# Swapping the row-group and slab axes of two masked operand tiles in a fused attention and expert block

## The chip, the cores and the metric

The kernel runs on one core of one Trainium2 chip. The metric is the device time of one execution in microseconds; of several executions the median counts. The core has TensorE (matmul), VectorE, ScalarE, GpSimd, and SyncE, whose queue issues all DMAs of this kernel.

## The reference

For 32 sequences of 128 tokens and width 128, the block computes a gated cross-attention and then a gated mixture of eight experts. Cut to what matters:

```
q = heads(layernorm(x) @ Wq.T + bq); k = heads(ctx @ Wk.T + bk); v = heads(ctx @ Wv.T + bv)   # 16 heads of 8
scores = einsum("bhqd,bhkd->bhqk", q, k) / sqrt(8);  scores = where(mask, min, scores)
x = x + tanh(g_xattn) * (softmax(scores) @ v merged over heads @ Wo.T + bo)
w = relu(softmax(n @ Wg + bg) - sigmoid(n @ Wt + bt) / 8), normalised      # n = layernorm(x)
x = x + tanh(g_ffn) * sum_e w_e * (gelu(n @ W1_e + b1_e) @ W2_e + b2_e)    # 8 experts, 512 hidden
```

## The kernel before

The program has two stages. The first (to about 290 us) does everything up to the gate; the second (290 us to the end) does the experts, with 512 tokens at a time as the moving operand, and the diff touches nothing in it.

The first stage is a software pipeline over 16 groups of two sequences (`GB = 2`, `GT = 256` tokens). `body(it)` on each engine handles several groups at different depths; `loop` runs some bodies unrolled, some in a hardware loop. The order of work on each engine is written out by hand, and semaphores are the only thing between engines.

Heads are only 8 wide, so four heads share one 128-row operand. The 16 heads are 4 slabs (`SLABS`, index s) of 4 row groups (`ROWS`, index r): head r of slab s lives in partitions 32r to 32r+31, which hold the high and low float parts of its 8 components in three copies, and some helper rows. The projections end in `k_stack` and `q_stack`, each [128 partitions, slab, 256 tokens] of 4 bytes, written by VectorE (L681). To get the scores of the four heads of a slab by one matmul, the operand is spread out with zeros: `k_masked` and `q_masked` hold, for each r, only partitions 32r to 32r+31 of the stack, the others stay zero. Both are [128, 4, 4, 256]: 16 KB in a partition.

The spreading is done by DMA from SBUF to SBUF, four DMAs per tile and group, one for each r: 32 partitions for `k_masked` (L380), 24 for `q_masked` (L395). Then one DMA copies `k_stack` to `k_cur` (L396). SyncE issues these in order: the `max_rows(1)` DMA of the current group (L359), the four `k_masked` copies of the next, the load of `ctx_sb` (L384), the four `q_masked` copies, `k_cur`, `max_rows(0)`, and the loads of the mask and of expert weights (L405, L408). The `k_masked` copies wait until VectorE has written `k_stack` and TensorE has read the former `k_masked`.

TensorE uses them in `natural` (L1002: `q_stack` of one slab as weights, `k_masked` as the moving operand with 4 blocks of 128 tokens; L1003 adds the mask) and `transposed` (L994: `k_cur` as weights, `q_masked` moving; L995 adds the mask). `natural` gives scores with the queries in partitions, only so that VectorE can take the negated maximum of each row (L654, into `neg_max`). `max_split` (L663, L665) cuts the 16 maxima into a high and a low part, TensorE transposes them, ScalarE copies them to `maxT`, and `max_rows` (L359) writes them as two rows of `q_masked`, so that `transposed` gives scores less the maximum, with keys in partitions, ready for the exponential (L546) and for `values` (L1013). For each group there are 8 `natural` and 8 `transposed` calls.

Of the kernel before, what the change touches and what calls it, by code (L numbers as in the profile page):

```python
# [25 lines left out]
F32 = mybir.dt.float32  # L26
F32R = mybir.dt.float32r
# [7 lines left out]
P = 128  # L35
B, S, D = 32, 128, 128
H, HD = 16, 8
E, FF = 8, 512
TOK = B * S
GB = 2  # L40
GT = GB * S
NG = B // GB
SLABS, ROWS = 4, 4
# [42 lines left out]
def group_at(it, ahead):  # L86

    if isinstance(it, int):
        g = it + ahead
        return g if 0 <= g < NG else None  # L90
    return it + ahead


def gated_block(nc, a):
# [3 lines left out]
    with ctx:  # L98
        def sb(name, shape, dt, stack=ctx):
            return stack.enter_context(nc.sbuf_tensor(name, shape, dt))  # L100

        def sem(name):
            return ctx.enter_context(nc.semaphore(name))
# [14 lines left out]

        def sa(name, shape, dt):
            return sb(name, shape, dt, phase_a)  # L120
        k_masked = sa("k_masked", [P, ROWS, SLABS, GT], F32R)
        q_masked = sa("q_masked", [P, ROWS, SLABS, GT], F32R)
        k_stack = sa("k_stack", [P, SLABS, GT], F32R)
        q_stack = sa("q_stack", [P, SLABS, GT], F32R)
        k_cur = sa("k_cur", [P, SLABS, GT], F32R)
# [28 lines left out]
        mean_var = sa("mean_var", [P, GB, 2], F32)  # L154
        rstd = sa("rstd", [P, GB], F32)
        power = sa("power", [P, B], F32)
        neg_max = sa("neg_max", [P, GB, ROWS, SLABS], F32)
        max_parts = sa("max_parts", [P, GB, 2 * H], F32R)
        maxT = sa("maxT", [2 * H, GT], F32R)
        headsT = sa("headsT", [P, GB, 2 * P], F32)  # L160
# [76 lines left out]
        km_in = sem("km_in")  # L237
        kcur_in = sem("kcur_in")
        qm_in = sem("qm_in")
        max_in = [sem("max0_in"), sem("max1_in")]  # L240
        maxhigh_done = [sem("max0_high_done"), sem("max1_high_done")]
# [41 lines left out]
        def settle(eng):  # L283

            eng.sem_inc(waited, 1)

        def misc_wait_full(eng, what, it):
            k = bank_of(what)
            eng.wait_ge(misc_full[k], fills(what, it))

        def misc_wait_read(eng, what, it):
            k = bank_of(what)
            eng.wait_ge(misc_read[k], fills(what, it))
# [8 lines left out]
        def wait_count(eng, s, n):  # L302
            if not (isinstance(n, int) and n <= 0):
                eng.wait_ge(s, n)

        def fill_of(group, b, s):

            return group * (GB * SLABS // 2) + (b * (SLABS // 2) + s // 2 + 1)
# [25 lines left out]
        def _(sp):  # L334
# [21 lines left out]
            sp.dma_start(x_all[:, 4 * GB:, :], a["x"][4 * GB * S:, :].rearrange("(b p) d -> p b d", p=P)).then_inc(x_rest_in, 16)  # L356

            def max_rows(b):
                sp.dma_start(q_masked[24:26, :, :, b * S:(b + 1) * S].rearrange("p r s q -> p (r s) q").bitcast(F32),  # L359
                             maxT[:, b * S:(b + 1) * S].bitcast(F32)).then_inc(max_in[b], 16)  # L360

            def body(it):
                if (g := group_at(it, 0)) is not None:
                    sp.wait_ge(maxT1_done, g + 1)
                    settle(sp)
                    max_rows(1)
                if (g := group_at(it, 1)) is not None:

                    misc_wait_read(sp, "p01", it - 1)
                    settle(sp)  # L370
                    misc_wait_read(sp, "p23", it - 1)
                    settle(sp)
                    if isinstance(g, int) and g == 0:
                        sp.wait_ge(pad_done, 2)
                    else:
                        sp.wait_ge(scoresN_full[1], fill_of(g - 1, GB - 1, SLABS - 1))
                        settle(sp)
                    for r in range(ROWS):
                        rows = slice(32 * r, 32 * r + 32)
                        sp.dma_start(k_masked[rows, r, :, :].bitcast(F32), k_stack[rows, :, :].bitcast(F32)).then_inc(km_in, 16)  # L380
                if (g := group_at(it, 3)) is not None and not (isinstance(g, int) and g == 0):
                    misc_wait_full(sp, "inputs", it)
                    settle(sp)
                    sp.dma_start(ctx_sb[:], ctx_v[g] if isinstance(g, int) else ctx_v[bass.ds(g, 1)]).then_inc(ctx_in, 16)  # L384
                if (g := group_at(it, 1)) is not None:
                    misc_wait_read(sp, "p45", it)
                    settle(sp)
                    misc_wait_read(sp, "p67", it)
                    settle(sp)
                    if not (isinstance(g, int) and g == 0):  # L390
                        sp.wait_ge(scoresT_full[1], fill_of(g - 1, GB - 1, SLABS - 1))
                        settle(sp)
                    for r in range(ROWS):
                        rows = slice(32 * r, 32 * r + 24)
                        sp.dma_start(q_masked[rows, r, :, :].bitcast(F32), q_stack[rows, :, :].bitcast(F32)).then_inc(qm_in, 16)  # L395
                    sp.dma_start(k_cur[:].bitcast(F32), k_stack[:].bitcast(F32)).then_inc(kcur_in, 16)  # L396
                    misc_wait_read(sp, "max0", it)
                    settle(sp)
                    max_rows(0)
                if (g := group_at(it, 2)) is not None and not (isinstance(g, int) and g == 0):  # L400
                    sp.wait_ge(masknxt_done, g)
                    settle(sp)
                    sp.wait_ge(maskcur_done, g)
                    settle(sp)
                    sp.dma_start(mask_words[:], mask_v[g] if isinstance(g, int) else mask_v[bass.ds(g, 1)]).then_inc(mask_in, 16)  # L405
                    sp.wait_ge(wsplit_done, g)
                    settle(sp)
                    sp.dma_start(w_raw[:], a["w_ffn"][g] if isinstance(g, int) else a["w_ffn"][bass.ds(g, 1)]).then_inc(w_in, 16)  # L408
            loop(sp, body)

            out_v = a["out"].rearrange("(g t p) d -> g p t d", p=P, t=TPB)
# [226 lines left out]
        def _(dve):  # L638
# [12 lines left out]

            def max_slab(group, b, s):
                dve.wait_ge(scoresN_full[s % 2], fill_of(group, b, s))
                nc.vector.tensor_reduce(neg_max[:, b, :, s],  # L654
                                        scores[:, 2 + s % 2, :].rearrange("p (r k) -> p r k", k=S),
                                        AX.X, ALU.max, negate=True).then_inc(scoresN_read[s % 2], 1)

            def max_split(group, b):

                for u in range(2):  # L660
                    dve.wait_ge(scoresN_read[u], fill_of(group, b, SLABS - 1))
                flat = neg_max[:, b, :, :].rearrange("p r s -> p (r s)")
                nc.vector.tensor_copy(max_parts[:, b, 0:H], flat).then_inc(maxhigh_done[b], 1)  # L663
                dve.wait_ge(maxhigh_done[b], group + 1)
                nc.vector.tensor_tensor(max_parts[:, b, H:2 * H], flat, max_parts[:, b, 0:H].bitcast(F32),  # L665
                                        ALU.subtract).then_inc(max_done[b], 1)

            def body(it):
# [90 lines left out]
                if (g := group_at(it, 1)) is not None:  # L759
                    max_slab(g, 1, 2)  # L760
                    max_slab(g, 1, 3)
                    max_split(g, 1)
# [96 lines left out]
        def _(pe):  # L859
            mm = nc.tensor.matmul  # L860

            def body(it):
# [26 lines left out]
                if (g := group_at(it, 0)) is not None:  # L889
                    transposed(g, 0, 2)  # L890
# [35 lines left out]
                if (g := group_at(it, 1)) is not None:  # L926
                    natural(g, 0, 2)
# [62 lines left out]
            def transposed(cur, b, s):  # L990

                wait_count(pe, scoresT_read[s % 2], fill_of(cur, b, s) - 1)
                dst = scores[:, s % 2, :].rearrange("p (r q) -> p r q", r=ROWS)
                mm(dst, k_cur[:, s, b * S:(b + 1) * S], q_masked[:, :, s, b * S:(b + 1) * S], start=True, stop=False)  # L994
                mm(dst, mask_cur[:, b, :], masked_ident[:].unsqueeze(1).to_broadcast([P, ROWS, P]),  # L995
                   start=False, stop=True).then_inc(scoresT_full[s % 2], 1)

            def natural(nxt, b, s):

                wait_count(pe, scoresN_read[s % 2], fill_of(nxt, b, s) - 1)  # L1000
                dst = scores[:, 2 + s % 2, :].rearrange("p (r k) -> p r k", r=ROWS)
                mm(dst, q_stack[:, s, b * S:(b + 1) * S], k_masked[:, :, s, b * S:(b + 1) * S], start=True, stop=False)  # L1002
                mm(dst, masked_ident[:], mask_nxt[:, b, :].unsqueeze(1).to_broadcast([P, ROWS, S]),  # L1003
                   start=False, stop=True).then_inc(scoresN_full[s % 2], 1)

# [129 lines left out]
```

## Time and profile before

| | us |
|---|---|
| median of 3 executions | 684.37 |
| lowest, highest | 682.66, 685.3 |
| the profiled execution, its own time | 685.3 |
| its span in the trace | 683.5 |
| TensorE busy in the span | 633.4 (93%) |
| VectorE busy | 532.4 (78%) |
| ScalarE busy | 432.8 (63%) |

The profile gives for each engine the busy time and, for each instruction, start, duration and what released it. Two cautions: a matmul's start is a record but its end is modelled, and neighbouring matmuls overlap, so that the rate of TensorE is read from the distance of starts a whole pattern apart, not from a mean duration. And a DMA row of SyncE's queue is the issuing only; the transfer lands later, and the views give that time apart.

### The profile page before, as it was taken

What the parts mean: (1) busy time and instruction counts of PE and PEld (TensorE: products, weight loads), DVE (VectorE), ACT (ScalarE), POOL (GpSimd) and SP (SyncE); (2) the same over time, 40 slices, a digit from 0 to 9 for tenths busy, and PEclk for the clock granted to TensorE, in tenths of its full rate; (3) what the DMA queues carried; (4) which work ended last, traced back from release to release, by engine and by line L of the source; (5) the groups of instructions that cost most, each with busy time, mean ns of one, the idle gap of its engine ahead of it and who ended that gap; (6) DMA issues with size and microseconds to landing.
All of it is one profiled execution on the core that took longest, in us unless ns stands there. A gap on an engine that the chain in (4) does not pass through costs nothing.

```text
span 683.5 us, 14449 instructions
## 1 busy us (share of the span) xinstructions
PE 633.4 (93%) x3944; PEld 478.2 (70%) x3944; DVE 532.4 (78%) x1083; ACT 432.8 (63%) x764; POOL 188.4 (28%) x242
## 2 busy tenths in 40 slices
PE   2899999999999999739999999999999999999996
PEld 2566666666666766427878878778788788787784
DVE  5778888899988888346877877868778778788686
ACT  3456666666666666418767757667576677675773
POOL 6224444444444443100230221212302202213022
PEclk9999999999999999959999999999999999999999
DMA  6544444444444444103121111111211211111110
GB/s 190 140 110 121 109 120 119 114 114 116 111 111 111 114 110 114 40 0 85 47 62 43 51 47 56 51 34 64 70 35 46 61 46 46 46 61 53 54 46 15
DMA packets 37386, 52.74 MB, mean 77 GB/s; under 512 B 9328, under 2 KB 20464, under 8 KB 37360
## 3 DMA queue, kind: packets, MB, share of 16 engines
q1 hardware_dynamic: 37360, 52.42, 27.8%
q8 instruction: 13, 0.21, 0.1%
q14 instruction: 13, 0.11, 0.1%
HBM read 26.58 MB, written 2.23 MB: 42 GB/s over the span
## 4 chain that ended last, share of the span: by engine, by line
PE 79%; DVE 8%; POOL 3%; DMA 3%; issue 2%; SPq 2%; ACT 2%; DVEq 0%; POOLq 0%; ACTq 0%
PE ps_y L1041 8%; PE ps_y L1043 8%; PE ps_y L1042 8%; PE ps_h L1061 8%; PE ps_h L1063 8%; PE ps_h L1062 8%; PE scores L994 5%; PE scores L995 4%; PE scores L1002 3%; PE scores L1003 3%; POOL yT L527 3%; DVE neg_max L654 3%; PE heads L1013 3%; PE misc L882 2%; PE misc L883 2%
## 5 line engine op out<-in xcount | busy, mean ns | idle before, releaser
L627 ACT ACTIVATE h_sb<-ps_h,b_sb 128x512 f32<-128x512 f32 x256 | 175.4, 689 | 116.2 <-PE ps_h L1063 103.6
L841 DVE TENSOR_TENSOR h_low<-h_sb,h_high 128x512 fp32r<-128x512 f32 x256 | 164.4, 682 | 0.0
L527 POOL TENSOR_TENSOR yT<-yT,weighted 128x512 f32<-128x512 f32 x56 | 72.3, 1292 | 309.2 <-DVE weighted L829 308.4
L837 DVE CAST h_high<-h_sb 128x512 fp32r<-128x512 f32 x128 | 86.8, 678 | 81.8 <-ACT h_sb L627 81.8
L1041 PE MATMUL ps_y<-h_high,w_high 128*128 128x512 f32 x256 | 102.2, 399 | 5.0 <-DVE h_low L841 5.0
L1061 PE MATMUL ps_h<-x_high,w_high 128*128 (+1 forms) x256 | 101.9, 398 | 0.1
L1043 PE MATMUL ps_y<-h_high,w_low 128*128 128x512 f32 x256 | 101.3, 396 | 0.0
L1042 PE MATMUL ps_y<-h_low,w_high 128*128 128x512 f32 x256 | 100.9, 394 | 0.0
L1063 PE MATMUL ps_h<-x_high,w_low 128*128 (+1 forms) x256 | 100.8, 394 | 0.0
L1062 PE MATMUL ps_h<-x_low,w_high 128*128 (+1 forms) x256 | 100.0, 391 | 0.0
L654 DVE TENSOR_REDUCE neg_max<-scores 128x4 f32<-128x512 f32 x128 | 83.6, 685 | 12.5 <-PE scores L1003 11.7
L632 ACT ACTIVATE h_high<-ps_h,b_sb 128x512 fp32r<-128x512 f32 x128 | 87.5, 684 | 0.0
L546 ACT ACTIVATE probs<-scores 128x512 f32<-128x512 f32 x128 | 72.9, 596 | 22.9 <-PE scores L995 20.6
L560 ACT ACTIVATE part<-misc,bqk_low,low_rows_sb 128x256 fp32r<-128x256 f32 x128 | 65.5, 565 | 34.5 <-PE misc L884 34.5
L1002 PE MATMUL scores<-k_masked,q_stack 128*128 128x512 f32 x128 | 63.6, 526 | 2.3 <-DMA k_masked<-k_stack 2.3
L994 PE MATMUL scores<-q_masked,k_cur 128*128 128x512 f32 x128 | 60.8, 503 | 4.4 <-DMA k_cur<-k_stack 1.9
L1041 PEld LDWEIGHTS ps_y<-h_high,w_high 128*128 128x128 f32 x256 | 48.0, 188 | 20.0 <-DVE h_low L841 5.6
L1061 PEld LDWEIGHTS ps_h<-x_high,w_high 128*128 128x128 f32 x256 | 48.5, 189 | 11.6 <-issue 0.5
L1062 PEld LDWEIGHTS ps_h<-x_low,w_high 128*128 128x128 f32 x256 | 48.5, 190 | 11.3
L1063 PEld LDWEIGHTS ps_h<-x_high,w_low 128*128 128x128 f32 x256 | 48.3, 188 | 11.1
L1043 PEld LDWEIGHTS ps_y<-h_high,w_low 128*128 128x128 f32 x256 | 48.1, 188 | 11.2
L1042 PEld LDWEIGHTS ps_y<-h_low,w_high 128*128 128x128 f32 x256 | 48.1, 188 | 9.8
(122 smaller groups left out, 990.7 us busy)
## 6 DMA issues: line engine op xcount, KB each, us to landing
w_row<-w_scratch SPq DMA_DIRECT2D x64, 256.0 KB, 3.2
k_masked<-k_stack SPq DMA_DIRECT2D x64, 128.0 KB, 2.4
k_cur<-k_stack SPq DMA_DIRECT2D x16, 512.0 KB, 3.0
q_masked<-q_stack SPq DMA_DIRECT2D x64, 96.0 KB
w_raw<-in_w_ffn SPq DMA_DIRECT2D x16, 256.0 KB, 2.7
ctx_sb<-in_ctx SPq DMA_DIRECT2D x16, 128.0 KB, 2.1
out_y<-y_out SPq DMA_DIRECT2D x8, 256.0 KB, 3.6
probs<-in_wqk SPq DMA_DIRECT2D x2, 256.0 KB, 3.1
```

What stands on the lines that cost most here:

```text
L527: nc.gpsimd.tensor_tensor(yT[:], yT[:], weighted[:, e % 2, :], ALU.add).then_inc(added, 1)
L627: nc.scalar.activation(h_sb[:, j % HBUF, :], ps_h[:, j % 4, :], ACT.Gelu_apprx_tanh, bias=b1_sb[:, j:j + 1]).then_inc(h_done, 1)
L632: nc.scalar.activation(h_high[:, j % HBUF, :], ps_h[:, j % 4, :], ACT.Gelu_apprx_tanh, bias=b1_sb[:, j:j + 1]).then_inc(high_even, 1)
L654: nc.vector.tensor_reduce(neg_max[:, b, :, s], scores[:, 2 + s % 2, :].rearrange("p (r k) -> p r k", k=S), AX.X, ALU.max, negate=True).the ...
L841: V.tensor_tensor(h_low[:, j % HBUF, :], h_sb[:, j % HBUF, :], h_high[:, j % HBUF, :].bitcast(F32), ALU.subtract).then_inc(low2_done, 1)
L994: mm(dst, k_cur[:, s, b * S:(b + 1) * S], q_masked[:, :, s, b * S:(b + 1) * S], start=True, stop=False)
L1041: mm(dst, w_high[:, E + e, cols], h_high[:, j % HBUF, :], start=(f == 0), stop=False)
L1042: mm(dst, w_high[:, E + e, cols], h_low[:, j % HBUF, :], start=False, stop=False)
L1043: mm(dst, w_low[:, E + e, cols], h_high[:, j % HBUF, :], start=False, stop=(f == FC - 1)).then_inc(w2_done, 1)
L1061: mm(dst, w_high[:, e, cols], xh, start=True, stop=False)
L1062: mm(dst, w_high[:, e, cols], xl, start=False, stop=False)
L1063: mm(dst, w_low[:, e, cols], xh, start=False, stop=True).then_inc(h_full, 1)
```

## The change

The two axes r and s of `k_masked` and `q_masked` change places: from [partition, r, s, token] to [partition, s, r, token]. Everything that indexes them follows: the spreading DMAs, the two matmuls, and `max_rows`. `neg_max` and so the order of the 16 maxima changes from (r, s) to (s, r), so that VectorE writes the four maxima of a slab side by side, and `max_rows` still writes 16 rows in the order of the tile. The alias `flat` in `max_split` goes, since `neg_max` is now flat.

For a matmul of slab s the four blocks of 128 tokens (512 bytes each) lay 4096 bytes apart and now lie 1024 bytes apart. For a spreading DMA the destination of one partition was one run of 4096 bytes and is now four runs of 1024 bytes, 4096 bytes apart; the source stays one run of 4096 bytes. No instruction is added, taken away or moved.

```diff
-        k_masked = sa("k_masked", [P, ROWS, SLABS, GT], F32R)
-        q_masked = sa("q_masked", [P, ROWS, SLABS, GT], F32R)
+        k_masked = sa("k_masked", [P, SLABS, ROWS, GT], F32R)
+        q_masked = sa("q_masked", [P, SLABS, ROWS, GT], F32R)
...
-        neg_max = sa("neg_max", [P, GB, ROWS, SLABS], F32)
+        neg_max = sa("neg_max", [P, GB, H], F32)
...
-                sp.dma_start(q_masked[24:26, :, :, b * S:(b + 1) * S].rearrange("p r s q -> p (r s) q").bitcast(F32),
+                sp.dma_start(q_masked[24:26, :, :, b * S:(b + 1) * S].rearrange("p s r q -> p (s r) q").bitcast(F32),
...
-                        sp.dma_start(k_masked[rows, r, :, :].bitcast(F32), k_stack[rows, :, :].bitcast(F32)).then_inc(km_in, 16)
+                        sp.dma_start(k_masked[rows, :, r, :].bitcast(F32), k_stack[rows, :, :].bitcast(F32)).then_inc(km_in, 16)
...
-                        sp.dma_start(q_masked[rows, r, :, :].bitcast(F32), q_stack[rows, :, :].bitcast(F32)).then_inc(qm_in, 16)
+                        sp.dma_start(q_masked[rows, :, r, :].bitcast(F32), q_stack[rows, :, :].bitcast(F32)).then_inc(qm_in, 16)
...
-                nc.vector.tensor_reduce(neg_max[:, b, :, s],
+                nc.vector.tensor_reduce(neg_max[:, b, ROWS * s:ROWS * s + ROWS],
...
-                flat = neg_max[:, b, :, :].rearrange("p r s -> p (r s)")
-                nc.vector.tensor_copy(max_parts[:, b, 0:H], flat).then_inc(maxhigh_done[b], 1)
+                nc.vector.tensor_copy(max_parts[:, b, 0:H], neg_max[:, b, :]).then_inc(maxhigh_done[b], 1)
...
-                mm(dst, k_cur[:, s, b * S:(b + 1) * S], q_masked[:, :, s, b * S:(b + 1) * S], start=True, stop=False)
+                mm(dst, k_cur[:, s, b * S:(b + 1) * S], q_masked[:, s, :, b * S:(b + 1) * S], start=True, stop=False)
...
-                mm(dst, q_stack[:, s, b * S:(b + 1) * S], k_masked[:, :, s, b * S:(b + 1) * S], start=True, stop=False)
+                mm(dst, q_stack[:, s, b * S:(b + 1) * S], k_masked[:, s, :, b * S:(b + 1) * S], start=True, stop=False)
```

On SyncE's queue, at the start of the second group's work, this is all that differs. The name before the arrow is what is written, the figures are partitions by the runs' dimensions, in elements of 4 bytes:

```order
-L380 DMA k_masked<-k_stack 32x1024 x4
+L380 DMA k_masked<-k_stack 32x4x256 x4
 L384 DMA ctx_sb<-in_ctx 128x2x128
-L395 DMA q_masked<-q_stack 24x1024 x4
+L395 DMA q_masked<-q_stack 24x4x256 x4
 L396 DMA k_cur<-k_stack 128x1024
 L359 DMA q_masked<-maxT 2x16x128
```

The order is the same; the spreading DMAs have become patterns of three dimensions, and the `max_rows` DMA has kept its form.

## Rows read from the trace of the kernel before

**Rows 1.** Page, part 1: busy time, share of the span, instructions of each engine.

```profile
PE 633.4 (93%) x3944; PEld 478.2 (70%) x3944; DVE 532.4 (78%) x1083; ACT 432.8 (63%) x764; POOL 188.4 (28%) x242
```

**Rows 2.** Busy time by stretches: projection-and-attention stage, expert stage; columns in the first line.

```profile
core 0: us, PE busy (x) PEld busy (x) DVE busy (x) ACT busy (x) POOL busy (x), PEclk, DMA share, GB/s
100.00:140.00 40.00, 39.40 (x365) 27.52 (x363) 35.43 (x94) 27.97 (x57) 16.19 (x25) 1.00 0.43 112
290.00:683.00 393.00, 368.90 (x1588) 294.09 (x1588) 295.66 (x481) 252.33 (x391) 73.77 (x58) 0.97 0.16 49
```

**Rows 3.** Page, part 5: groups of instructions; last numbers are busy us, mean ns.

```profile
L841 DVE TENSOR_TENSOR h_low<-h_sb,h_high 128x512 fp32r<-128x512 f32 x256 | 164.4, 682 | 0.0
...
L1061 PE MATMUL ps_h<-x_high,w_high 128*128 (+1 forms) x256 | 101.9, 398 | 0.1
...
L654 DVE TENSOR_REDUCE neg_max<-scores 128x4 f32<-128x512 f32 x128 | 83.6, 685 | 12.5 <-PE scores L1003 11.7
...
L1002 PE MATMUL scores<-k_masked,q_stack 128*128 128x512 f32 x128 | 63.6, 526 | 2.3 <-DMA k_masked<-k_stack 2.3
L994 PE MATMUL scores<-q_masked,k_cur 128*128 128x512 f32 x128 | 60.8, 503 | 4.4 <-DMA k_cur<-k_stack 1.9
```

**Rows 4.** TensorE in order of time, attention: start us, duration us, engine, line.

```profile
120.35 0.50 PE L994 MATMUL scores<-q_masked,k_cur 128*128 128x512 f32 x1
120.69 0.39 PE L995 MATMUL scores<-masked_ident,mask_cur 128*128 128x512 bf16 x1
120.73 0.58 PE L1002 MATMUL scores<-k_masked,q_stack 128*128 128x512 f32 x1
121.16 0.39 PE L1003 MATMUL scores<-mask_nxt,masked_ident 128*128 128x512 bf16 x1
121.20 0.58 PE L1002 MATMUL scores<-k_masked,q_stack 128*128 128x512 f32 x1
...
122.58 0.58 PE L1002 MATMUL scores<-k_masked,q_stack 128*128 128x512 f32 x1
```

**Rows 5.** TensorE in order of time, expert stage, same columns.

```profile
499.98 0.39 PE L1061 MATMUL ps_h<-x_high,w_high 128*128 x1
500.21 0.39 PE L1062 MATMUL ps_h<-x_low,w_high 128*128 x1
...
505.50 0.39 PE L1061 MATMUL ps_h<-x_high,w_high 128*128 x1
```

**Rows 6.** Time line of the same iteration, the rows of SyncE's DMA queue.

```profile
116.16 2.48 SPq L380 DMA_DIRECT2D k_masked<-k_stack  x4
...
126.93 0.69 SPq L359 DMA_DIRECT2D q_masked<-maxT  x1
```

**Rows 7.** Line 380, k_masked copies: issue ns min/median/max, and below landings.

```profile
L380 SPq DMA_DIRECT2D k_masked<-k_stack x64: 562/582/649, 17.1 to 265.1; - x64
...
DMA to landing us min/median/max: 2.3/2.4/3.7
```

**Rows 8.** Time line of a later iteration: SyncE's copies and the matmul that needs them.

```profile
263.20 2.46 SPq L380 DMA_DIRECT2D k_masked<-k_stack  x4
...
267.61 0.58 PE L1002 MATMUL scores<-k_masked,q_stack 128*128 128x512 f32 x1
```

**Rows 9.** Waits, 20 to 280 us: waiter <- awaited: us total, times, longest.

```profile
PE scores L1002 <- DMA k_masked<-k_stack: 2.3, 2, 1.7
...
PE scores L994 <- DMA k_cur<-k_stack: 1.9, 2, 1.1
```

**Rows 10.** Chain that ended last, first 60 us: start us, us, what.

```profile
17.06 0.65 SPq L380
...
19.02 2.44 DMA k_masked<-k_stack
...
34.01 3.73 DMA k_masked<-k_stack
...
39.99 0.81 SPq L395
...
43.16 3.52 DMA k_cur<-k_stack
...
47.07 0.47 PE scores L994
```

**Rows 11.** Issues of lines 395, 396, 408, 427: ns min/median/max, first and last start.

```profile
L395 SPq DMA_DIRECT2D q_masked<-q_stack x64: 713/725/1722, 20.5 to 272.3; - x64
...
L396 SPq DMA_DIRECT2D k_cur<-k_stack x16: 532/535/552, 23.7 to 273.0; - x16
...
L408 SPq DMA_DIRECT2D w_raw<-in_w_ffn x15: 345/346/532, 28.8 to 259.1; - x15
...
L427 SPq DMA_DIRECT2D out_y<-y_out x7: 406/407/431, 368.6 to 646.1; - x7
```

**Rows 12.** DMA view of 117.0 to 119.0 us: only k_masked copies under way.

```profile
DMA packets 120, 0.36 MB, mean 180 GB/s; under 512 B 32, under 2 KB 32, under 8 KB 120
...
q1 hardware_dynamic: 120, 0.36, 80.0%
```

**Rows 13.** DMA view of 127.0 to 128.1 us: mostly the k_cur copy.

```profile
DMA packets 89, 0.32 MB, mean 287 GB/s; under 512 B 12, under 2 KB 12, under 8 KB 89
...
q1 hardware_dynamic: 89, 0.32, 82.9%
```

**Rows 14.** DMA view of 119.8 to 122.5 us: the ctx_sb load, 512-byte rows.

```profile
DMA packets 289, 0.14 MB, mean 50 GB/s; under 512 B 32, under 2 KB 288, under 8 KB 289
...
q1 hardware_dynamic: 289, 0.14, 17.6%
```

**Rows 15.** Page, part 6: DMA issues: count, KB each, median us to landing.

```profile
k_cur<-k_stack SPq DMA_DIRECT2D x16, 512.0 KB, 3.0
```

**Rows 16.** Time line at a k_cur copy and its first matmul.

```profile
126.21 0.54 SPq L396 DMA_DIRECT2D k_cur<-k_stack  x1
...
130.20 0.47 PE L994 MATMUL scores<-q_masked,k_cur 128*128 128x512 f32 x1 [0.17 <-issue]
```

More of the change, by code:

```diff
@@ L661, in max_split @@
                     dve.wait_ge(scoresN_read[u], fill_of(group, b, SLABS - 1))
-                flat = neg_max[:, b, :, :].rearrange("p r s -> p (r s)")
-                nc.vector.tensor_copy(max_parts[:, b, 0:H], flat).then_inc(maxhigh_done[b], 1)
+                nc.vector.tensor_copy(max_parts[:, b, 0:H], neg_max[:, b, :]).then_inc(maxhigh_done[b], 1)
                 dve.wait_ge(maxhigh_done[b], group + 1)
-                nc.vector.tensor_tensor(max_parts[:, b, H:2 * H], flat, max_parts[:, b, 0:H].bitcast(F32),
+                nc.vector.tensor_tensor(max_parts[:, b, H:2 * H], neg_max[:, b, :], max_parts[:, b, 0:H].bitcast(F32),
                                         ALU.subtract).then_inc(max_done[b], 1)
```

## The prediction

> **What bounds the kernel now.** Part 1 of the page gives TensorE 93% of the span, VectorE 78% [rows 1]. The busy time by stretches then splits this: in the first stage TensorE shows 39.40 of 40 us busy at the full granted clock (1.00), in the expert stage 368.90 of 393, and no line of the expert stage is touched [rows 2]. So whatever the change does is done before 290 us, and there it counts if it alters how fast TensorE streams, or makes it wait.
>
> The costliest groups hold a lure. The matmul that reads `k_masked` is given with a mean of 526 ns and the one that reads `q_masked` with 503, while a matmul of the same 512 columns in the expert stage, whose moving operand is one plain run, has 398 [rows 3]. Both slow ones are just those whose operand the change packs closer. But ends are modelled, so the rate has to be read from starts. In the attention stage a pair (masked operand, then mask) starts at 120.73, 121.20, ... 122.58: four pairs in 1.85 us, 0.462 us a pair [rows 4]. In the expert stage 24 matmuls start from 499.98 to 505.50: 0.230 us each, 0.460 for two [rows 5]. The blocks 4096 bytes apart therefore stream as fast as a plain run; the 526 ns is a start that is logged early, 0.04 us behind the mask matmul, and waits in the pipe.
>
> The third view is SyncE's queue beside TensorE. Four `k_masked` copies are issued from 116.16 on for 2.48 us, so the last starts near 118.04 [rows 6]; landing takes 2.4 us in the median [rows 7], hence 120.44. The first matmul that needs them starts at 120.73 [rows 4]: a slack of 0.29 us. From first issue to that matmul it is 4.57 us here; over the 14 groups behind the start-up it is about that in twelve, and 4.41 in the two tightest, of which one is shown, 263.20 to 267.61 [rows 8]: a slack of 0.13. The views of waits say the same from the other side: only 2 waits on these copies, 2.3 us in all, and 2 on `k_cur` [rows 9]. Those lie in the start-up, where the chain that ended last goes through the copies three times: 17.06 to 21.46, 32.15 to 37.74, and 39.99 to 46.68 with `k_cur` behind the `q_masked` copies [rows 10].
>
> **The change part by part.** *The matmuls* (128 of each kind): at most they could gain the 0.0025 us by which a pair is slower than two plain ones, x256 = 0.6 us, less than what two decimals can carry; a loss has no reason, since a plain run (block distance 512 bytes) and a distance of 4096 stream alike and 1024 lies between. I take 0.
>
> *VectorE's reduction*: it wrote 4 maxima 16 bytes apart and now side by side. It takes 685 ns; a subtraction that writes 512 elements in a run takes 682 [rows 3]. What the scatter costs is 3 ns, x128 = 0.4 us at most, and only a part of it is waited for. `max_split` reads and writes 16 values in a run before and after, and the `max_rows` DMA keeps its form. I take 0 for these.
>
> *The spreading DMAs* (64 + 64) are what really changes: a partition's 4096 bytes go in four runs of 1024. Two terms, the issue and the transfer.
>
> Issue: 0.582 us for a `k_masked` copy [rows 7]. The nearest rows on runs: a load with one run of 2 KB in each of 128 partitions takes 346 ns to issue, the store of four runs of 512 bytes each 406 [rows 11]: 384 more runs for 0.06 us. Upward the slowest form of this kernel is the 24-partition copy with 725 ns [rows 11], whose length I can't lay to runs. `max_rows` was issued in 0.69 [rows 6] with 32 runs of 512 bytes, 0.11 above. Downward, the 128-partition copy with 4 KB runs takes 535 and the one with 2 KB runs 346, so that shorter runs might save 0.19. I take +0.06, nearest in what differs; the ends are -0.19 and +0.11. Three issues lie ahead of the last: +0.18 us.
>
> Transfer: over 117.0 to 119.0 us the 16 engines are 80.0% busy and move 120 packets, 32 of them the small ones under 512 bytes: 0.80 x 16 x 2.0 us / 88 = 0.29 us for 4 KB [rows 12]. With `k_cur`, over all 128 partitions, it is 0.829 x 16 x 1.1 / 77 = 0.19 us [rows 13]. A copy within 32 partitions is thus held by something other than the engine itself. Pieces of 512 bytes take 0.176 x 16 x 2.7 / 257 = 0.030 us [rows 14], so 4 KB in eight such pieces 0.24, and in four of 1 KB at most that. Against 0.19 this is up to +0.05 for each row of 4 KB; an engine has two rows (32 partitions over 16 engines), +0.10 a copy, and if two engines that wait for each other both pay it, +0.19. If the pieces fit under the 0.29 that a row takes anyway, it is 0. I take +0.05, the middle of 0 and the plain +0.10. It doesn't add up over the four copies while issuing (0.64) is slower than moving (0.58 + 0.05). By the same row a faster issue would bring little: with 0.39 the engines, at 0.58 a copy, become the limit, so the batch ends 3 x 0.04 = 0.12 us earlier at the most.
>
> What the Trainium skill makes of these terms stands by itself. [...] The rule that speaks against the change is in the Trainium skill's "Perfetto Trace Analysis", section "Optimizing DMA Performance": large descriptors are what matters where DMA binds. [...] "SBUF — State Buffer" of the Trainium skill, section "Door 1: The DMA port swizzle", gives 32 partitions only 8 of 16 ports; the trace agrees (0.29 us for 4 KB against 0.19).
>
> **The sum.** The last copy lands x = 0.18 + 0.05 = 0.23 us later. In 12 steady groups that is under the slack of 0.29: 0. In two it exceeds 0.13 by 0.10: +0.2. In the start-up the chain runs through three batches: 3 x 0.23 = +0.7. `k_cur` in steady state: it lands 3.0 us after its issue [rows 15], so that the one of 126.21 is there at 129.2, and its matmul starts at 130.20 [rows 16]; four slower issues ahead (0.24) stay hidden. VectorE's writing of the next stacks comes far behind. Total +0.9 us on the profiled execution's 685.3, that is 686.2; the median of the runs stands 0.9 below that execution, so the forecast for the median is **685.3 us**. Bounds: x = -0.12 gives -0.4 (684.0); x = 0.33 + 0.19 = 0.52 gives 12 x 0.23 + 2 x 0.39 + 3 x 0.52 = +5.1 (689.5).
>
> **The rivals.** (1) *Late copies slow every iteration*: the mechanism just priced, past its threshold. Cost is 17x - 3.7 for x above 0.29, so it passes 0.5% (3.4 us) at x = 0.42, and with x = 0.52 the time is **689.5**. For it: a steady slack of only 0.29, engines 80% busy in the batch, and no steady wait that would absorb a delay of TensorE. Against: both terms must stand near their upper ends. Should issuing go to 725 ns, x is 0.43 + 0.10, much the same time. (2) *The masked matmuls really are slowed by the distance of their blocks*, and fall to 398 ns: 128 x 128 ns + 128 x 105 ns = 29.8 us, **654.6**. For it only the means; against it the starts, which leave nothing to gain. (3) *The DMAs get cheaper*, because long runs were what made issuing slow (535 against 346 ns): the transfers then bind, -0.4 us, **684.0**, which can't be told from no change. That the change doesn't do what it says is excluded, as SyncE's order shows the new forms.
>
> **How the numbers follow.** About 0.5% (3.4 us) is what a measurement of this kernel can tell from no change. The forecast (x between 0 and 0.42, 684.4 to 687.8) has 0.67, the cheaper DMAs 0.14, late copies 0.13, faster matmuls 0.04, and 0.02 for something unseen, split evenly. So faster 0.05, same 0.81, slower 0.14. The range runs from 682.5, the cheaper DMAs less the 1.7 us by which the lowest run stands under the median, to 689.0, most of the late-copies case; the matmul case is left out.
>
> **What would show it.** Starts of pairs 0.46 us apart as before, with the means of L1002 and L994 about where they are; packets of 1 KB in place of 4 KB, some 10,700 more in all; L380's issue near 0.64 us and landings at 2.4 to 2.5; iterations of 16.34 us as before (the nine from 116.16 to 263.20, [rows 6, 8]). New steady waits of L1002 on the `k_masked` copies would show rival 1; a pair under 0.45 us, rival 2; issuing under 0.5 us, rival 3. The forecast is wrong if the distance of blocks acts on something that starts of matmuls don't show, or if a copy of four runs is issued in another way than the rows compared here.

## The result and the profile after

The changed kernel is slower: a median of 689.77 us against 683.51, a ratio of 1.0091 with a 95% interval of 1.0068 to 1.0113. That is +6.3 us where +0.9 was forecast, and beyond the upper end of the range, 689.0.

Page of the changed kernel, part 5 (groups, mean ns after the busy time) and part 6 (DMA issues, last number the median landing). They answer to [rows 3, 15]:

```profile
L1060 PE MATMUL ps_h<-x_high,w_high 128*128 (+1 forms) x256 | 101.7, 397 | 0.0
...
L654 DVE TENSOR_REDUCE neg_max<-scores 128x4 f32<-128x512 f32 x128 | 83.7, 685 | 14.2 <-PE scores L1002 13.1
...
L993 PE MATMUL scores<-q_masked,k_cur 128*128 128x512 f32 x128 | 60.7, 503 | 8.4 <-issue 4.7
L1001 PE MATMUL scores<-k_masked,q_stack 128*128 128x512 f32 x128 | 62.9, 521 | 3.6 <-DMA k_masked<-k_stack 3.6
...
k_masked<-k_stack SPq DMA_DIRECT2D x64, 128.0 KB, 2.5
k_cur<-k_stack SPq DMA_DIRECT2D x16, 512.0 KB, 3.1
```

The line numbers of this file are one lower behind line 662, so that L1001 and L1002 are `natural`, L993 and L994 `transposed`. The matmuls take what they took (521 and 503 ns against 526 and 503), the reduction too (685). What has grown most is the idle time of TensorE before L993: 8.4 us where it was 4.4. Its largest part, 4.7 us, carries the name "issue", that is, no releaser that the trace could name. In the kernel before, that part was 0.5 us, as the view of the attention lines has it:

```profile
L994 PE MATMUL scores<-q_masked,k_cur 128*128 128x512 f32 x128 | 60.8, 503 | 4.4 <-DMA k_cur<-k_stack 1.9 <-DMA q_masked<-maxT 0.9 <-issue 0.5
```

The issue times of the copies, from the views of lines 380, 395 and 396 of the changed kernel (ns min/median/max), answer to [rows 7, 11]:

```profile
L380 SPq DMA_DIRECT2D k_masked<-k_stack x64: 587/612/757, 17.2 to 269.8; - x64
```

```profile
L395 SPq DMA_DIRECT2D q_masked<-q_stack x64: 778/788/1800, 20.7 to 278.9; - x64
...
L396 SPq DMA_DIRECT2D k_cur<-k_stack x16: 554/558/567, 24.1 to 279.7; - x16
```

The time line of one steady iteration of the changed kernel (start us, duration us; SPq is SyncE's DMA queue, PEld TensorE's weight load, which starts with its matmul or just ahead of it), to be laid beside [rows 4, 6, 16]:

```profile
116.98 2.61 SPq L380 DMA_DIRECT2D k_masked<-k_stack  x4
...
121.77 0.19 PEld L1001 LDWEIGHTS scores<-k_masked,q_stack 128*128 128x128 f32 x1 [0.18 <-issue]
...
123.99 3.39 SPq L395 DMA_DIRECT2D q_masked<-q_stack  x4
...
127.43 0.56 SPq L396 DMA_DIRECT2D k_cur<-k_stack  x1
...
128.18 0.68 SPq L359 DMA_DIRECT2D q_masked<-maxT  x1
...
131.36 0.19 PEld L993 LDWEIGHTS scores<-q_masked,k_cur 128*128 128x128 f32 x1 [0.46 <-issue]
...
132.60 0.67 SPq L359 DMA_DIRECT2D q_masked<-maxT  x1
...
133.78 0.66 SPq L380 DMA_DIRECT2D k_masked<-k_stack  x1
```

The same iteration of the kernel before, weight loads and issues that the rows ahead don't show:

```profile
120.70 0.19 PEld L1002 LDWEIGHTS scores<-k_masked,q_stack 128*128 128x128 f32 x1
...
123.03 3.14 SPq L395 DMA_DIRECT2D q_masked<-q_stack  x4
...
130.17 0.19 PEld L994 LDWEIGHTS scores<-q_masked,k_cur 128*128 128x128 f32 x1 [0.23 <-issue]
...
131.40 0.67 SPq L359 DMA_DIRECT2D q_masked<-maxT  x1
...
132.59 0.57 SPq L380 DMA_DIRECT2D k_masked<-k_stack  x1
```

Cut at five of these events, an iteration reads as follows (us, each stretch the difference of two starts):

| stretch | before | after |
|---|---|---|
| first `k_masked` issue to its first matmul's weight load | 4.54 | 4.79 |
| to the first `q_masked` issue | 2.33 | 2.22 |
| to the `max_rows(0)` issue | 3.90 | 4.19 |
| to the first `q_masked` matmul's weight load | 3.24 | 3.18 |
| to the next `k_masked` issue | 2.42 | 2.42 |
| iteration | 16.43 | 16.80 |

The events follow one another in a ring: the first `q_masked` matmul is followed by the issue of `max_rows(1)` after 1.23 us (1.24 in the changed kernel), and that by the next `k_masked` batch after 1.19 (1.18). Two stretches grew, +0.25 at the `k_masked` batch, of which 0.11 is given back in the next stretch, and +0.29 in the `q_masked` batch; the others differ by 0.06 at most. Over nine iterations the mean went from 16.37 us (`k_masked` issues from 83.36 to 230.67) to 16.81 (83.39 to 234.64), 0.44 us more each.

Laid over the whole profile, the account is this. Up to the third `k_masked` batch (49.63 us before, 49.03 after) the changed kernel was 0.6 us ahead; over the 13 iterations from there to the last batch (263.20 and 267.82) it lost 5.2 us; behind that batch it lost another 1.7, and this makes the 6.3 us between the spans. So the steady loss is most of it, 0.40 us an iteration with the last ones. The first and the last part hold one late landing each, of which more below.

### The profile page after: what moved, and what is told of

Its sections match the earlier page's. It is cut to its first block, busy times and chain, and to the rows that moved or that the text cites. A ratio compares the mean times of both kernels' runs of the same rounds, so it can differ in the third digit from the quotient of the medians.

```text
span 689.8 us, 14449 instructions
## 1 busy us (share of the span) xinstructions
PE 635.0 (92%) x3944; PEld 479.0 (69%) x3944; DVE 534.3 (77%) x1083; ACT 432.7 (63%) x764; POOL 188.1 (27%) x242
## 3 DMA queue, kind: packets, MB, share of 16 engines
HBM read 26.58 MB, written 2.23 MB: 42 GB/s over the span
## 4 chain that ended last, share of the span: by engine, by line
PE 79%; DVE 8%; issue 3%; POOL 3%; DMA 3%; SPq 2%; ACT 2%; DVEq 0%; POOLq 0%; ACTq 0%
PE ps_y L1040 8%; PE ps_y L1042 8%; PE ps_y L1041 8%; PE ps_h L1062 8%; PE ps_h L1060 8%; PE ps_h L1061 8%; PE scores L993 5%; PE scores L994 4%; PE scores L1001 4%; PE scores L1002 3%; POOL yT L527 3%; DVE neg_max L654 3%; PE heads L1012 3%; PE misc L881 2%; PE misc L882 2%
## 5 line engine op out<-in xcount | busy, mean ns | idle before, releaser
L993 PE MATMUL scores<-q_masked,k_cur 128*128 128x512 f32 x128 | 60.7, 503 | 8.4 <-issue 4.7
L1001 PE MATMUL scores<-k_masked,q_stack 128*128 128x512 f32 x128 | 62.9, 521 | 3.6 <-DMA k_masked<-k_stack 3.6
```

The costliest lines, as they stand in the source:

```text
L993: mm(dst, k_cur[:, s, b * S:(b + 1) * S], q_masked[:, s, :, b * S:(b + 1) * S], start=True, stop=False)
L1001: mm(dst, q_stack[:, s, b * S:(b + 1) * S], k_masked[:, s, :, b * S:(b + 1) * S], start=True, stop=False)
```

## The experiments

All kernels below were timed in five rounds beside the kernel before, whose median was 682.78 us beside e1 to e4, 683.12 beside e5 to e8 and 683.55 beside e9 and e10; differences and ratios are to these. The theories at the start: both batches arrive late and each costs something (theory T), or one of them alone (rivals K and Q), or the matmuls stream slower (rival M). A mean iteration is again that of nine in the steady loop.

**One operand at a time.** e1 gives the new order to `k_masked` only (the index of its matmul, left out here, follows):

```diff
-        k_masked = sa("k_masked", [P, ROWS, SLABS, GT], F32R)
+        k_masked = sa("k_masked", [P, SLABS, ROWS, GT], F32R)
...
-                        sp.dma_start(k_masked[rows, r, :, :].bitcast(F32), k_stack[rows, :, :].bitcast(F32)).then_inc(km_in, 16)
+                        sp.dma_start(k_masked[rows, :, r, :].bitcast(F32), k_stack[rows, :, :].bitcast(F32)).then_inc(km_in, 16)
```

> The kernel before, with the new axis order for k_masked alone. Theory T (both batches of copies come late: the k_masked batch lands beyond its slack by some 0.2 us an iteration, and the max_rows(0) DMA, queued behind the slower q_masked batch, by another 0.2): about half of the 6.3 us, 686 to 687.5. Rival Q (the delay comes from the q_masked batch alone, since the 0.29 us of slack before the k_masked matmul still covers it): no change in the steady iterations, 683.5 to 684.5. Rival K (the k_masked batch alone): 689 to 690. Rival M (the matmuls stream slower at 1024 bytes distance, not the DMAs): half of it, and pairs of matmuls more than 0.46 us apart.

Measured: 686.08 us, ratio 1.0045 (1.0028 to 1.0062). e2 is the complement:

> The changed kernel with k_masked put back to the old axis order: only q_masked (and the order of the maxima) is new. Theory T: the other half, 686 to 687.5, with the idle time before the first q_masked matmul of a group near 0.4 us where it was 0.17. Rival Q: all of it, 689 to 690. Rival K: 683.5 to 684.5. If both batches simply queue behind one another and either alone is absorbed, e1 and e2 together fall short of 6.3 us.

Measured: 688.96 us, ratio 1.0087 (1.0071 to 1.0103). Neither is nothing, so both theories of one batch alone fall; but e2 is above what theory T gave it. The `q_masked` batch by itself costs nearly as much as both together in time, and the two don't add up (+3.3 and +6.2 us against +6.3). The time line of an iteration of e2:

```profile
151.32 2.47 SPq L380 DMA_DIRECT2D k_masked<-k_stack  x4
...
155.88 0.19 PEld L1001 LDWEIGHTS scores<-k_masked,q_stack 128*128 128x128 f32 x1
...
158.20 3.44 SPq L395 DMA_DIRECT2D q_masked<-q_stack  x4
...
162.42 0.67 SPq L359 DMA_DIRECT2D q_masked<-maxT  x1
...
165.58 0.19 PEld L993 LDWEIGHTS scores<-q_masked,k_cur 128*128 128x128 f32 x1 [0.49 <-issue]
```

The first stretch is that of the kernel before (4.56), the `q_masked` batch has all the growth (158.20 to 162.42, 4.22 for 3.90), and the matmul follows `max_rows(0)` after 3.16 us, as in the changed kernel. In e1 it is the other way round: 4.85 in the first stretch, 3.94 in the third. Mean iterations: 16.58 (e1), 16.70 (e2), 16.81 (both), that is +0.21 and +0.33 against +0.44. Here too the parts come to more than the whole, by 0.10 us; why is open.

**A plain run for the moving operand, shorter runs for the DMA.** e3 is the changed kernel with the following edit; the spreading DMA, left out here, follows it with eight runs of 512 bytes in a partition:

```diff
-        k_masked = sa("k_masked", [P, SLABS, ROWS, GT], F32R)
+        k_masked = sa("k_masked", [P, SLABS, GB, ROWS, S], F32R)
...
-                mm(dst, q_stack[:, s, b * S:(b + 1) * S], k_masked[:, s, :, b * S:(b + 1) * S], start=True, stop=False)
+                mm(dst, q_stack[:, s, b * S:(b + 1) * S], k_masked[:, s, b, :, :], start=True, stop=False)
```

> The changed kernel with k_masked laid out as slab, sequence, row group, token: the moving operand of a k_masked matmul is one plain run of 512 elements, and a partition's row is copied in eight runs of 512 bytes. If pieces cost time (theory T), the k_masked batch issues and lands still later by about as much as from one run to four, 0.1 to 0.4 us an iteration: 691 to 695. If the distance of blocks in the moving operand costs anything, the pairs of L1001 and L1002 get closer than 0.46 us and the time falls to under 689. If neither, 689.8.

Measured: 696.01 us, ratio 1.0187 (1.0163 to 1.0212), a little above the expected 691 to 695. TensorE's time line of e3 has, where the operand is one run of 512 elements:

```profile
126.03 0.58 PE L1001 MATMUL scores<-k_masked,q_stack 128*128 128x512 f32 x1
...
127.42 0.58 PE L1001 MATMUL scores<-k_masked,q_stack 128*128 128x512 f32 x1
```

Three pairs in 1.39 us, 0.463 a pair: the same as with blocks 4096 bytes apart (0.462), and as in the changed kernel, where they are 1024 apart and three pairs take 1.38 us:

```profile
122.16 0.58 PE L1001 MATMUL scores<-k_masked,q_stack 128*128 128x512 f32 x1
...
123.54 0.58 PE L1001 MATMUL scores<-k_masked,q_stack 128*128 128x512 f32 x1
```

With that the rival of matmuls slowed by the distance is out. The landings of line 380 in e3, after 2.4/2.5/4.3 in the changed kernel and [rows 7] before:

```profile
DMA to landing us min/median/max: 2.5/2.8/4.4
```

Issuing hardly grew from four runs to eight (median 612 to 619 ns), landing did by 0.3 us, and the first stretch went to between 5.10 and 5.19. The mean iteration is 17.16. So shorter runs make the transfer's end later as well; at four runs it was 0.1.

**Taking the queue in front of max_rows(0) away.** e4 (changed kernel) and e5 (kernel before) have the one edit

```diff
+                    sp.dma_start(k_cur[:].bitcast(F32), k_stack[:].bitcast(F32)).then_inc(kcur_in, 16)
                     for r in range(ROWS):
                         rows = slice(32 * r, 32 * r + 24)
...
-                    sp.dma_start(k_cur[:].bitcast(F32), k_stack[:].bitcast(F32)).then_inc(kcur_in, 16)
```

> The changed kernel with the k_cur copy issued ahead of the four q_masked copies, so that the max_rows(0) DMA is no longer queued behind its 512 KB. Theory T: max_rows(0) and the last q_masked copy land earlier, the idle time before the first q_masked matmul goes, and the share of the q batch (about 3 us) comes back: 685.5 to 687.5. Rival K: nothing changes, 689.8. If k_cur's 512 KB only push the q_masked copies back by as much, nothing changes either, but then the idle time stays.

Measured: 682.85 us, ratio to the kernel before 0.9996 (0.9982 to 1.0011): more than expected, the whole loss is gone. The mean iteration is 16.39.

> The kernel before with k_cur issued ahead of the q_masked copies. If the first q_masked matmul of a group was waiting for max_rows(0) already in the kernel before (3.1 to 3.2 us from that issue to the matmul in every kernel that shows an idle time there), the wait shrinks a little and the time falls by what it was late, 0 to 0.2 us an iteration: 680.5 to 683. If there was a slack there, nothing changes: 683.

Measured: 680.32 us, ratio 0.9951 (0.9932 to 0.9970), by a hair below the range that a late gate was given. The kernel before was thus itself held up at this wait. e5's time line:

```profile
120.69 0.51 SPq L393 DMA_DIRECT2D k_cur<-k_stack  x1
121.25 3.15 SPq L396 DMA_DIRECT2D q_masked<-q_stack  x4
...
124.58 0.68 SPq L359 DMA_DIRECT2D q_masked<-maxT  x1
...
127.50 0.19 PEld L994 LDWEIGHTS scores<-q_masked,k_cur 128*128 128x128 f32 x1
```

From the `max_rows(0)` issue to the weight load it is now 2.92 us, and 2.64 in e4, with no idle time ahead; in the steady iterations of every kernel that has idle time there it is 3.1 to 3.3. The time from issue to readiness is thus 3.1 to 3.3 us behind `k_cur`'s 512 KB, and at most 2.64 without them. In the last group of the kernel before `max_rows(1)` goes out with no large copy ahead of it, and there the trace does name it as what the matmul waits for; the chain that ended last gives its landing:

```profile
278.14 2.26 DMA q_masked<-maxT
```

The views don't give this landing for `max_rows(0)` in the steady loop, nor those of the `q_masked` copies. That the wait is for `max_rows(0)` and not for the last of these copies is argued: in e5 the copies go out later behind the first `k_masked` matmul than in the kernel before (2.87 us against 2.33), `max_rows(0)` at the same distance (6.20 against 6.23), and the `q_masked` matmul comes 0.35 us earlier. In either case it is the 512 KB of `k_cur` that hold the matmul up. The iteration of e5 is 16.18 us.

**Delaying without touching a layout.** e6 and e7 are the kernel before with four increments of a semaphore that nobody waits for, ahead of one batch:

```diff
+                    for _ in range(4):
+                        settle(sp)
                     for r in range(ROWS):
```

> The kernel before with SyncE held up by four semaphore increments (an estimated 0.2 to 0.28 us, from the 0.05 to 0.07 us between such rows) ahead of each k_masked batch; layouts and transfers as before. The slack of 0.29 us that the prediction read: no steady change, 683 to 684. Slack of 0.05 or less, because the waits and register work that follow the wait for the copies in the loop take the rest: 0.15 to 0.25 us an iteration, 685.5 to 687, and from the batch's first issue to the matmul about 4.56 us as before, with the whole iteration longer.

Measured: 686.47 us, ratio 1.0047 (1.0032 to 1.0062).

> The same four increments ahead of each q_masked batch. Zero slack at max_rows(0): 0.2 to 0.28 us in each of 15 iterations, 686 to 688, with the idle time before the first q_masked matmul near 0.45 us. A slack of a microsecond, as the prediction had it from k_cur's landing: 683.

Measured: 688.20 us, ratio 1.0069 (1.0047 to 1.0091), 0.2 above the range. The time line of e6, ahead of and behind a `k_masked` batch:

```profile
150.49 2.46 SPq L382 DMA_DIRECT2D k_masked<-k_stack  x4
...
155.02 0.19 PEld L1004 LDWEIGHTS scores<-k_masked,q_stack 128*128 128x128 f32 x1 [0.15 <-issue]
...
157.24 3.13 SPq L397 DMA_DIRECT2D q_masked<-q_stack  x4
```

The batch now follows the first `q_masked` matmul of the group before after 2.67 us where it was 2.42, a delay of 0.25; the `k_masked` matmul still comes 4.53 us behind the batch, so it moved by the full 0.25: no slack at this gate. The following stretch gave 0.11 back (2.22 for 2.33), just as in the changed kernel, and the mean iteration is 16.51, +0.14.

The 0.11 us are a slack one step further on. In all nine iterations of the kernel before, the `q_masked` batch goes out 6.87 to 6.89 us behind the `k_masked` batch, whether the matmul between them came after 4.54 us or after 4.67: something other than this matmul released it. In the changed kernel and in e6 it goes out 2.21 to 2.23 us behind the matmul each time, which has become the later of the two. What the other one is, no run here shows.

e7 in the same way:

```profile
149.34 2.48 SPq L380 DMA_DIRECT2D k_masked<-k_stack  x4
...
156.44 3.13 SPq L397 DMA_DIRECT2D q_masked<-q_stack  x4
...
160.33 0.69 SPq L359 DMA_DIRECT2D q_masked<-maxT  x1
...
163.47 0.19 PEld L996 LDWEIGHTS scores<-q_masked,k_cur 128*128 128x128 f32 x1 [0.37 <-issue]
```

The `q_masked` batch goes out 7.10 us behind the `k_masked` batch, 0.22 later than before, and this comes through whole: the mean iteration is 16.59, +0.22, with 3.14 us from `max_rows(0)` to the matmul and 0.37 us idle ahead of it. Both matmuls stood without slack in the kernel before. This is shown without a layout, a run length or a matmul being different.

**What lies between landing and matmul.** e8 is the changed kernel with

```diff
-                    pe.wait_ge(km_in, g * (ROWS * 16) + ROWS * 16)
                     misc_wait_read(pe, "p45", it)
                     misc_wait_read(pe, "p67", it)
                     pe.wait_ge(masknxt_done, g + 1)
+                    pe.wait_ge(km_in, g * (ROWS * 16) + ROWS * 16)
...
-                    pe.wait_ge(max_in[0], g * 16 + 16)
                     pe.wait_ge(maskcur_done, g + 1)
+                    pe.wait_ge(max_in[0], g * 16 + 16)
```

> The changed kernel with two waits of TensorE moved, each behind the other waits of its group: the one for the k_masked copies to just ahead of their first matmul, and the one for max_rows(0) behind that for the mask. If the register work of the waits behind them is what lies between landing and matmul (about 0.28 us at k_masked), some 0.1 to 0.25 us an iteration come back: 686 to 688.5. If the time after landing is the DMA's own (the semaphore's travel), nothing changes: 689.8.

Measured: 690.38 us, ratio 1.0105 (1.0083 to 1.0128): no gain, a miss. One iteration of e8:

```profile
134.14 2.62 SPq L380 DMA_DIRECT2D k_masked<-k_stack  x4
...
138.77 0.19 PEld L1001 LDWEIGHTS scores<-k_masked,q_stack 128*128 128x128 f32 x1
...
141.03 3.39 SPq L395 DMA_DIRECT2D q_masked<-q_stack  x4
...
145.21 0.68 SPq L359 DMA_DIRECT2D q_masked<-maxT  x1
...
148.47 0.19 PEld L993 LDWEIGHTS scores<-q_masked,k_cur 128*128 128x128 f32 x1 [0.55 <-issue]
```

The first stretch fell from 4.79 to 4.63, so the three waits that followed, with their register work, were worth 0.16 us between landing and matmul. But the second took 0.04 of it back (2.26 for 2.22): the `q_masked` batch is again 6.89 us behind the `k_masked` batch, where the other release holds it. And the fourth grew by 0.08 (3.26 for 3.18), for a reason that no run shows. The mean iteration is 16.72 where it was 16.81, a gain that the timing doesn't resolve.

e9 and e10 put only the wait for the `k_masked` copies last, and issue `k_cur` first, on either layout:

> The kernel before with k_cur issued ahead of the q_masked copies (as in e5) and TensorE's wait for the k_masked copies put behind the three other waits of its place. e8 shortened the stretch from the first k_masked issue to its matmul from 4.80 to 4.63 us, but lost it again at max_rows(0). With the max_rows(0) wait out of the way, a gate at k_masked that still binds would let 0.1 to 0.15 us an iteration through: 678 to 679.5. If TensorE's own work is what fills the iteration of 16.19 us in e5, nothing changes: 680.3.

Measured: 679.57 us, ratio 0.9949 (0.9935 to 0.9963). That lies between the two cases of the expectation, but the interval is that of e5 and the iteration is 16.19 us for 16.18: nothing beyond e5 is shown.

> The changed kernel with both edits. e4 stands at 682.85 with 4.85 us from issue to matmul. If k_masked's gate binds there, the moved wait gives back about 0.17 us an iteration: 680 to 681. If both layouts then run alike (within 0.5% of the kernel with the same edits and the old layout), the whole cost of the new layout was in the two gates and none in the matmuls.

Measured: 681.47 us, ratio 0.9958 (0.9938 to 0.9977), 0.5 us above the range, and below e4, whose interval (0.9982 to 1.0011) this one doesn't reach. So with the first `q_masked` matmul relieved, the `k_masked` gate of the new layout still cost something in e4 (its matmul idles 0.20 to 0.28 us each time, and the iteration is 16.39), and the moved wait took it off. The `k_masked` batches follow each other in e9 and e10 like this:

```profile
112.26 2.46 SPq L380 DMA_DIRECT2D k_masked<-k_stack  x4
...
128.45 2.47 SPq L380 DMA_DIRECT2D k_masked<-k_stack  x4
```

```profile
112.82 2.61 SPq L380 DMA_DIRECT2D k_masked<-k_stack  x4
...
129.01 2.62 SPq L380 DMA_DIRECT2D k_masked<-k_stack  x4
```

16.19 us an iteration in both, with batches that take 2.46 and 2.61 us to issue. Once neither gate is late, the two layouts have the same iteration, and their times can't be told apart (0.9949 and 0.9958, the intervals overlap). Over such an iteration TensorE is busy 16.05 of 16.19 us in e9 and 16.04 in e10, and no view names a wait of it; that its own chain is what is left fits this, but no run tries it. The lowest times of the study are those of e5 and e9, on the old layout, 0.5% below the kernel before; between the two no difference is shown.

## Why the prediction was wrong

*The matmuls* (0): right. Pairs are 0.46 us apart with three distances of blocks, 4096 and 1024 bytes and, in e3, 512.

*The reduction and the maxima* (0): right, 685 ns as before.

*The terms of x*: roughly right. A `k_masked` copy is issued in 612 ns, +0.03 where +0.06 was taken; a `q_masked` copy in 788, +0.063. Landing is +0.1 where +0.05 was taken. At the matmul the whole was +0.22 in the mean of nine iterations (4.81 us for 4.59), against x = 0.23.

*The slack of 0.29 us at the `k_masked` matmul*: wrong; it was none. The step laid the landing (2.4 us after issue) against the start of the matmul. But TensorE has three more waits with their register work between the wait for the copies and the matmul; moving them ahead took 0.16 us off (e8), and a delay of 0.25 reached the matmul whole (e6). Those 0.16 account for about half of the 0.29; what fills the rest is not shown. The two groups that the prediction called the tightest, with 4.41 us instead of 4.57, show that the matmul can come that early. Their batches, at 49.63 and 263.20, belong to unrolled bodies of the loop, where the waits are for constants and need no register work; that this is why is likely, not shown, since a third unrolled group (246.82) took 4.72. Of each lateness here 0.11 us is given back one stretch later, so that the cost was 0.1 to 0.2 us an iteration (e6, e1) and not 0.

*"`k_cur` in steady state ... four slower issues ahead (0.24) stay hidden"*: this is the step that carries most of the error. For `k_cur` it is true, but the matmul waits for `max_rows(0)` too, which is issued behind `k_cur` and whose landing no view gives in the steady loop. It was named in no term, and the step read a slack of 1 us where there was none. The sign was there: [rows 16] end in "0.17 <-issue", an idle time with no releaser, and the matmul's weight load comes 3.24 us behind that DMA's issue; the same 3.1 to 3.3 us go with the idle times of the experiments. This gate had no slack (e7, and e5 which gained 2.8 us by relieving it), and 4 x 0.063 plus 0.02 of a slower `k_cur` issue are 0.27 of the 0.29 us by which the batch grew. The new layout of `q_masked` alone costs 6.2 us (e2).

*The start-up* (+0.7): neither seen nor excluded. The third `k_masked` batch was issued at 49.03 us in the profile after and at 49.63 before. What blurs this is a late landing in each profiled execution, 3.7 us at 34.01 before [rows 10], where 2.4 is the median, and 4.3 at 269.82 after (the matmul idles 1.81 us for it). Such a landing comes and goes with either layout: the last `k_masked` matmul idles 1.2 to 1.8 us in the profiles of e1, e2, e4, e5, e7 and e8 too, and not in those of the kernel before, e6, e9 and e10. So the profiled executions can't price this term.

*Rival 1*, late copies in every iteration, is what happened, at 689.77 where it was priced 689.5. That its price came out right is luck: x was under its threshold of 0.29, the threshold was not there, and the second gate was not in it. Given 0.13, it should have been the forecast. Rivals 2 and 3 are out: no pair got closer, and no issue got shorter.

## What to carry to other kernels

In a software pipeline that goes round through several engines, read slack at each wait and not at one: list every DMA that a matmul waits for, those too whose landing the profile doesn't give, and take an idle time whose releaser is missing as a sign that such a one may bind. Slack is what a deliberate small delay shows, not landing against the start of the next instruction, since the waits behind it can take time of their own (0.16 us here). And when several copies are issued in a row, try whether the one that is waited for last should not stand behind the largest: moving a 512 KB copy four places up was worth 2.8 us on the old layout, and 6.2 on the new one (+6.3 against +0.1), about all that the layout cost.

## What was not expected of the hardware

Cutting a copy into shorter runs didn't make the DMA engines busier for a KB. Over the batch of the changed kernel, 117.6 to 121.7 us, the DMA view has

```profile
DMA packets 618, 0.55 MB, mean 133 GB/s; under 512 B 64, under 2 KB 618, under 8 KB 618
...
q1 hardware_dynamic: 618, 0.55, 59.7%
```

0.597 x 16 x 4.1 us = 39.2 us of engine time went to 512 pieces of 1 KB, 42 of 512 bytes of the next load (1.3 us at 0.030) and 64 small ones, which are left out here as in the prediction. That is 74 ns for each KB; the 4 KB pieces had 0.29 us, 73 ns for each KB. Still the copies landed 0.1 us later, and 0.3 us more with pieces of 512 bytes. What fills that time is open: the engines were not busy with it, and whether their descriptors come more slowly no run here shows.

A `q_masked` copy of 24 partitions takes longer to issue than one of 32 (725 against 582 ns), and its four runs cost it twice as much (63 against 30 ns). Why is open as well.
